# One more probability slot, a down block one score batch later, and a later tangent in a fused attention and mixture-of-experts layer

## The chip, the cores and the metric

The kernel runs on one core of a Trainium2 chip. Its metric is the device time of one launch in microseconds. Before the change it was 2091.04 us (median of 3 runs, 2090.17 to 2092.35).

## What is computed

`x` has 4096 tokens of 256 numbers. `xn` is its layer norm. The output is `x` plus two branches that both read `xn`:

```
# attention, 16 heads of 16
energy = einsum('bqhd,bkhd->bhqk', q, k)          # 4096 x 4096 for each head
attn   = softmax(energy / sqrt(256))
out    = einsum('bhqk,bkhd->bqhd', attn, v)
# feed-forward: one shared expert and, for each token, the best 2 of 8
expert(t) = silu((t @ w1 + b1) * (t @ w3 + b3)) @ w2 + b2      # hidden width 352
```

## The kernel before

**Two streams on one order.** After a front part of about 95 us (norm, projections, routing), TensorE (PE below) runs one order, written out by hand, in which attention and feed-forward are interleaved.

*Attention.* A "group" is one key tile of 128 against 1024 queries: `scores` (L900) issues two matmul instructions for it that fill two of the eight PSUM banks. There are 2048 groups. ScalarE (ACT) takes the exponential of a group from PSUM into one slot of the ring `probs` in SBUF (L1206). A "value step" (`values`, L913) multiplies the two groups of one key tile by the head's values; there are 1024. The scores of three groups fit in PSUM at a time (`SB = 3`, six banks), so the scores of group n wait until group n-3 has left PSUM. For most groups that is the end of exponential n-3. For the places in `MOVED` VectorE (DVE) copies the scores to the slot (L1784), which frees PSUM, and ACT then takes the exponential in place in SBUF (L1198). At the places in `MERGED` one instruction of ACT takes two groups (L1203).

*Feed-forward.* It is cut into 55 "units" of up to 256 tokens: 8 shared, 39 routed, 8 shared. Unit u has three "up" blocks of 12 matmuls (`up_both`, L925), each with two products for a part of the hidden width; DVE adds biases and multiplies them (L1669, L1674). ACT takes one tangent for the unit (`tanh`, L1183), DVE makes `hid` (L1679) and splits it in a rounded part and its rest (L1684 to L1691), and the "down" block (`down_tile`, L937, 18 matmuls) belongs to the next unit's stretch of the order. DVE then takes the result from PSUM (`keep`, L1733 or L1739) and splits the next weights (L1696 to L1708).

**The order of a unit.** `unit(u)` (L1004) has twelve "batches" of three groups' scores. Numbered from 0, batch b holds the places 3b to 3b+2 of the unit. Behind each stands one "gap" of other work. Before the change the gaps are:

batch 0, up; 1, three value steps; 2, up; 3, three value steps; 4, **down of the unit before**; 5, two value steps; 6, two; 7, two; 8, up; 9, two; 10, two; 11, two.

The last group of batches 0, 2 and 5 to 11 is a moved one (`MOVED = (2, 8, 17, 20, ...)`). The groups of batches 1, 3 and 4 are not moved, so the third score of batch 5, place 17, waits for exponential 14. The tangent stands on ACT behind the exponential of place `TANH_AT` - 36 = 5 of the next unit. Units 0 and 1 have no moved and no merged groups, nor do the groups ahead of unit 0 and behind unit 54.

**Slots.** A value step reads two slots, and the slot of a group is written again only when PE has passed its value step. With `NPB = 8` at most eight groups are between scores and values; `FIRST_VALUES` and `FIRST_GROUPS` set the lead at a unit's start.

**Boundaries.** After each 32 value steps the output bank is full: DVE transposes it away (`take_output`, L1628), and the next value step waits for that; two value steps later it adds the result to `resid` (`add_output`, L1633 to L1640). As 18 steps go to a unit, the boundary falls on another place in each: behind `stop` = -(FIRST_VALUES + 18u) mod 32 value steps of unit u, if that is at most 18.

PE, ACT and DVE each run their own list in order, with semaphores between them; none passes a waiting instruction.

## Time and profile before

| | us |
|---|---|
| runs, median (range) | 2091.04 (2090.17 to 2092.35) |
| profiled execution, its own time | 2090.63 |
| its span in the trace | 2088.7 |
| PE, ACT, DVE busy | 2060.6, 2001.1, 1376.5 |
| granted TensorE clock, mean | 1.00 of 2.4 GHz |

The profile is one execution. The page gives busy time by engine, the chain that ended last, and the costliest groups of instructions. The timeline gives each instruction's start and duration from the span's start; equal neighbours are merged in a row (x3). A value step is eight rows of L913 in the trace (x24 is three steps), and a batch of scores is six of L900. How long a block holds PE is read from its start to the start of the next block, since durations overlap.

### The profile page before, as it was taken

How to read it: one execution, taken by the hardware profiler on the slowest of the kernel's cores; microseconds unless marked ns; L12 is line 12 of the kernel's file. 1: busy time of each engine (PE TensorE's matmuls, PEld its weight loads, DVE VectorE, ACT ScalarE, POOL GpSimd, SP SyncE). 2: the span in 40 equal slices, each digit the busy share in tenths (PEclk: the TensorE clock that was granted, in tenths of full speed). 3: DMA queues.
4: the chain of work that ended last, by engine and by line, in shares of the span. 5: the costliest groups of instructions: out<-in, count | busy, mean ns of one | idle time of the engine just before them, and what ended most of it. 6: DMA issues, size and time to landing. Idle time of an engine off the chain costs nothing.

```text
span 2088.7 us, 38791 instructions
## 1 busy us (share of the span) xinstructions
PE 2060.6 (99%) x15722; PEld 968.7 (46%) x15722; DVE 1376.5 (66%) x2038; ACT 2001.1 (96%) x2122; POOL 253.1 (12%) x260
## 2 busy tenths in 40 slices
PE   8999999999999999999999999999999999999998
PEld 6734444444444444444444444444444444444442
DVE  8554666576766666767676767666767665677772
ACT  6799999999999999999999999999999999999998
POOL 0306764000000000000000000000000000033320
PEclk9999999999999999999999999999999999999999
DMA  8874443222231213132222231313132222132322
GB/s 291 287 255 118 119 135 105 61 54 74 60 81 51 79 52 85 52 80 60 66 60 74 62 79 52 86 47 81 52 81 60 73 60 68 57 113 82 112 66 68
DMA packets 223354, 187.83 MB, mean 90 GB/s; under 512 B 110471, under 2 KB 192190, under 8 KB 223174
## 3 DMA queue, kind: packets, MB, share of 16 engines
q1 hardware_dynamic: 209350, 148.68, 25.5%
q0 software_dynamic: 12496, 36.34, 5.4%
q8 instruction: 124, 2.03, 0.4%
q14 instruction: 56, 0.46, 0.1%
q10 hardware_dynamic: 1328, 0.33, 0.1%
HBM read 130.21 MB, written 55.05 MB: 89 GB/s over the span
## 4 chain that ended last, share of the span: by engine, by line
PE 84%; ACT 10%; DVE 4%; DMA 1%; issue 1%; SPq 0%; DVEq 0%; ACTq 0%
PE PS L913 40%; PE PS L900 26%; PE PS L925 12%; ACT probs L1206 6%; PE PS L937 6%; ACT probs L1198 2%; ACT probs L1203 1%; DVE probs L1784 1%; DMA qk_parts<-part_a 1%; DVE stats L1332 0%; DVE probs L1356 0%; DVE o_t L1628 0%; DVE x_parts L1368 0%; PE PS L804 0%; DMA resid<-in_x 0%
## 5 line engine op out<-in xcount | busy, mean ns | idle before, releaser
L1206 ACT ACTIVATE probs<-PS 128x1024 f32<-128x1024 f32 x1359 | 1311.8, 1051 | 49.4 <-PE PS L900 48.4
L913 PE MATMUL PS<-probs,v_head 128*32 128x512 f32 x8192 | 984.5, 599 | 8.4 <-DVE o_t L1628 4.4
L1784 DVE COPY probs<-PS 128x1024 f32<-128x1024 f32 x477 | 583.5, 1223 | 451.3 <-PE PS L900 450.1
L900 PE MATMUL PS<-q_ring,k_stack 50*128 50x512 f32 x4096 | 676.2, 431 | 7.9 <-ACT probs L1206 3.6
L900 PEld LDWEIGHTS PS<-q_ring,k_stack 50*128 50x128 f32 x4096 | 335.0, 184 | 482.7 <-ACT probs L1206 315.0
L1198 ACT ACTIVATE probs<-probs 128x1024 f32<-128x1024 f32 x477 | 517.4, 1085 | 1.5 <-DVE probs L1784 0.8
L913 PEld LDWEIGHTS PS<-probs,v_head 128*32 128x32 f32 x8192 | 210.7, 109 | 521.7 <-issue 391.7
L1203 ACT ACTIVATE probs<-PS 128x2048 f32<-128x2048 f32 x106 | 201.3, 1899 | 0.2 <-PE PS L900 0.2
L925 PE MATMUL PS<-x_hi,w_hi 128*128 128x256 f32 (+9 forms) x660 | 199.2, 302 | 0.0
L1278 POOL DMA_DIRECT2D slot_y<-y_sb x39 | 27.9, 716 | 1378.4 <-DVE y_sb L1739 1342.9
L925 PE MATMUL PS<-x_hi,w_lo 128*128 128x256 f32 (+9 forms) x660 | 184.1, 279 | 0.0
L925 PE MATMUL PS<-x_lo,w_hi 128*128 128x256 f32 (+9 forms) x660 | 183.6, 278 | 0.0
L925 PEld LDWEIGHTS PS<-x_hi,w_hi 128*128 128x128 f32 (+1 forms) x660 | 118.7, 180 | 59.6 <-issue 59.6
L1669 DVE TENSOR_SCALAR gate_in<-PS,bias_sb 128x256 f32<-128x256 f32 (+7 forms) x165 | 76.8, 466 | 90.6 <-PE PS L925 89.1
L925 PEld LDWEIGHTS PS<-x_lo,w_hi 128*128 128x128 f32 (+1 forms) x660 | 118.9, 180 | 0.0
L925 PEld LDWEIGHTS PS<-x_hi,w_lo 128*128 128x128 f32 (+1 forms) x660 | 118.9, 180 | 0.0
L937 PE MATMUL PS<-w_hi,hid_hi 128*128 128x256 f32 (+4 forms) x318 | 95.6, 301 | 0.0
L1700 DVE TENSOR_TENSOR w_lo<-w_raw,w_hi 128x1408 fp32r<-128x1408 f32 x55 | 89.4, 1626 | 1.9
L937 PE MATMUL PS<-w_hi,hid_lo 128*128 128x256 f32 (+4 forms) x318 | 89.7, 282 | 0.0
L937 PE MATMUL PS<-w_lo,hid_hi 128*128 128x256 f32 (+4 forms) x318 | 89.6, 282 | 0.0
L1674 DVE SCALAR_TENSOR_TENSOR prod<-PS,bias_sb,gate_in 128x256 f32<-128x256 f32 (+7 forms) x165 | 76.9, 466 | 5.9
L1269 POOL DMA_INDIRECT slot_x<-y_sb,pos x64 | 67.6, 1056 | 19.1 <-issue 14.6
...
## 6 DMA issues: line engine op xcount, KB each, us to landing
...
```

What stands on the lines that cost most here:

```text
L900: last = pe.matmul(bank(2 * score_buffer(turn, g) + r), k_stack[rows, kt * P:(kt + 1) * P], q_ring[rows, sweep, i * QC:(i + 1) * QC], star ...
L913: last = pe.matmul(bank(O_BANK)[VW * j:VW * (j + 1), :], v_head[:, kt, :], probs[:, slot, (j % 2) * QC:(j % 2 + 1) * QC], start=(kt == 0), ...
L925: last = pe.matmul(f_half(w)[0:FT[j], 0:width(u)], a[u % 2][:, w, dt, j * P:j * P + FT[j]], b[:, dt * CH:dt * CH + width(u)], start=(n == ...
L937: last = pe.matmul(f_half(t)[0:own, :], a[0:rows, j, t * P:t * P + own], b[0:rows, j, :], start=(n == 0), stop=(n == 8))
L1198: nc.scalar.activation(probs[:, prob_slot(g), :], probs[:, prob_slot(g), :], ACT.Exp, scale=ENERGY_SCALE).then_inc(s_exp, 1)
L1203: nc.scalar.activation(pair, bank(2 * score_buffer(h, g), 4), ACT.Exp, scale=ENERGY_SCALE).then_inc(s_exp, 2)
L1206: nc.scalar.activation(probs[:, prob_slot(g), :], bank(2 * score_buffer(h, g), 2), ACT.Exp, scale=ENERGY_SCALE).then_inc(s_exp, 1)
L1269: nc.gpsimd.indirect_dma_start(out=slot_x, out_offset=bass.IndirectOffsetOnAxis(ap=pos[:, u * TPU + t, k:k + 1], axis=0), in_=rows[:, t, : ...
L1669: V.tensor_scalar(gate_in[0:FT[j], 0:width(u)], f_half(0)[0:FT[j], 0:width(u)], bias_sb[0:FT[j], u % 2, j:j + 1], 0.5, ALU.add, ALU.mult). ...
L1674: V.scalar_tensor_tensor(prod[u % 2][0:FT[j], j, 0:width(u)], f_half(1)[0:FT[j], 0:width(u)], bias_sb[0:FT[j], u % 2, 3 + j:4 + j], gate_i ...
L1700: V.tensor_tensor(w13_lo[u % 2][:, :, :, :], w13_raw[:, :, :, :], w13_hi[u % 2][:, :, :, :].bitcast(f32), ALU.subtract).then_inc(s_w13, 1)
L1784: V.tensor_copy(probs[:, prob_slot(g), :], bank(2 * score_buffer(h, g), 2)).then_inc(s_moved, 1)
```

## The change

`NPB` goes from 8 to 9, and the unit begins three groups ahead of twice its value steps instead of two (`FIRST_VALUES` 12, `FIRST_GROUPS` 27). The ring is indexed by a running number; its ninth slot lies in a tile of its own, `probs_8`. The SBUF for it comes from `prod`, whose two buffers now share their middle part, and from `gate_in`, which goes: the first product of an up block is written to its place in `prod` and multiplied there.

The gaps of a unit become: batch 0, up; 1, three value steps; 2, up; 3, three; 4, **two value steps**; 5, **down**; 6, two; 7, two; 8, up; 9, two; 10, two; 11, two. `long_gaps` gives other numbers where a boundary falls behind the second step (two behind batch 1, one behind the up of batch 2, three) or behind the fourth (four, none, two). The tangent goes from behind place 5 to behind place 11, and DVE's list is put in another order. `MOVED` and `MERGED` stay as they are.

```diff
-NPB = 8
+NPB = 9
...
-FIRST_VALUES = 14
-FIRST_GROUPS = 2 * FIRST_VALUES + 2
+FIRST_VALUES = 12
+FIRST_GROUPS = 2 * FIRST_VALUES + 3
 UNIT_VALUES = 18
 UNIT_GROUPS = 2 * UNIT_VALUES
-TANH_AT = 41
+TANH_AT = 47
 MOVED = (2, 8, 17, 20, 23, 26, 29, 32, 35)
 MERGED = (27, 30)
...
+def part_at(u, j):
+
+    return j if u % 2 else (j + 1) % 3
+
+
+def long_gaps(u):
+
+    stop = -(FIRST_VALUES + u * UNIT_VALUES) % NT
+    return (2, 1, 3) if stop == 2 else (4, 0, 2) if stop == 4 else (3, 0, 3)
...
-    return g % NPB
+def prob_slot(n):
+
+    return n % NPB
...
-        probs = sb("probs", [P, NPB, 2 * QC], f32)
+        probs = sb("probs", [P, NPB - 1, 2 * QC], f32)
...
-        gate_in = sb("gate_in", [P, CH], f32)
-        prod = [sb(f"prod{b}", [P, 3, CH], f32) for b in range(2)]
+        prod = sb("prod", [P, 5, CH], f32)
         hid = sb("hid", [P, 3, CH], f32)
+        probs_8 = sb("probs_8", [P, 2 * QC], f32)
...
+        def prob_at(n):
+
+            return probs[:, prob_slot(n), :] if prob_slot(n) < NPB - 1 else probs_8[:, :]
+
+        def prod_of(u):
+
+            return prod[:, 0:3, :] if u % 2 else prod[:, 2:5, :]
...
+                first, late, second = long_gaps(u)
                 next_scores(3)
                 up_both(u, 0)
                 next_scores(3)
-                next_values(3)
+                next_values(first)
                 next_scores(3)
                 up_both(u, 1)
+                next_values(late)
                 next_scores(3)
-                next_values(3)
+                next_values(second)
+                next_scores(3)
+                next_values(2)
                 next_scores(3)
                 if u == 0:
                     count_choices()
                 down_tile(u - 1, 0)
                 down_tile(u - 1, 1)
-                next_scores(3)
-                next_values(2)
                 next_scores(3)
                 next_values(2)
                 next_scores(3)
...
-            next_scores(1)
+            next_scores(2)
...
-            next_scores(1)
...
-                V.tensor_scalar(gate_in[0:FT[j], 0:width(u)], f_half(0)[0:FT[j], 0:width(u)], bias_sb[0:FT[j], u % 2, j:j + 1], 0.5,
+                V.tensor_scalar(prod_of(u)[0:FT[j], part_at(u, j), 0:width(u)], f_half(0)[0:FT[j], 0:width(u)], bias_sb[0:FT[j], u % 2, j:j + 1], 0.5,
                                 ALU.add, ALU.mult).then_inc(s_gin, 1)
...
+                take_values(m + 4)
                 move_scores(u, 8)
                 if real:
                     gate(u, 1)
                     product(u, 1)
-                if u:
-                    hidden(u - 1)
-                take_values(m + 4)
-                if u:
-                    hidden_hi(u - 1)
-                    hidden_lo(u - 1)
-                take_values(m + 6)
                 after_values(m + 4)
                 if more:
                     up_hi(u + 1)
+                take_values(m + 6)
+                if u:
+                    hidden(u - 1)
+                    hidden_hi(u - 1)
+                    hidden_lo(u - 1)
+                take_values(m + 8)
+                move_scores(u, 17)
+                if more:
                     up_lo(u + 1)
                 if u == 0:
                     dve.wait_ge(s_pre, 1)
@@ -1823,12 +1844,10 @@
                     dve.wait_ge(s_prc, 1)
                 else:
                     keep(u - 1)
-                move_scores(u, 17)
                 after_values(m + 6)
+                move_scores(u, 20)
                 if real:
                     down_hi(u)
-                take_values(m + 8)
```

What this moves, for a unit of 256 tokens (unit 31's down block). On PE, where the unit's second gap of three value steps (x12 here, four instructions to a step) and the down block stand, before:

```order
L900 MATMUL PS<-q_ring,k_stack 128x512 x6
L913 MATMUL PS<-probs,v_head 32x512 x12
L900 MATMUL PS<-q_ring,k_stack 128x512 x6
L937 MATMUL PS<-w_hi,hid_hi 128x256
L937 MATMUL PS<-w_lo,hid_hi 128x256
```

and now:

```order
L918 MATMUL PS<-q_ring,k_stack 128x512 x6
L931 MATMUL PS<-probs,v_head 32x512 x12
L918 MATMUL PS<-q_ring,k_stack 128x512 x6
L931 MATMUL PS<-probs,v_head 32x512 x8
L918 MATMUL PS<-q_ring,k_stack 128x512 x6
L955 MATMUL PS<-w_hi,hid_hi 128x256
L955 MATMUL PS<-w_lo,hid_hi 128x256
```

The down block (first row with `hid_hi`) now has one more gap, of two value steps, and one more batch of scores ahead of it.

On ACT, around the tangent (`hid<-prod`), from a moved exponential (`probs<-probs`, place 35 of the unit before) on, before:

```order
L1198 ACTIVATE probs<-probs 128x1024
L1206 ACTIVATE probs<-PS 128x1024 x3
L1183 ACTIVATE hid<-prod 128x768
L1206 ACTIVATE probs<-PS 128x1024 x2
L1198 ACTIVATE probs<-probs 128x1024
L1206 ACTIVATE probs<-PS 128x1024 x8
L1198 ACTIVATE probs<-probs 128x1024
```

and now:

```order
L1217 ACTIVATE probs<-probs 128x1024
L1225 ACTIVATE probs<-PS 128x1024 x5
L1217 ACTIVATE probs<-probs 128x1024
L1225 ACTIVATE probs<-PS 128x1024 x3
L1202 ACTIVATE hid<-prod 128x768
L1225 ACTIVATE probs<-PS 128x1024 x5
L1217 ACTIVATE probs<-probs 128x1024
```

The tangent goes from between exponentials 5 and 6 to between 11 and 12.

On DVE, from the second up block's product on (before) or from the split of the next up weights on (now), before:

```order
L1674 SCALAR_TENSOR_TENSOR prod<-PS,bias_sb,gate_in 128x256
L1679 SCALAR_TENSOR_TENSOR hid<-hid,prod 128x768
L1684 CAST hid_hi<-hid 128x512
L1685 CAST hid_hi<-hid 96x256
L1690 TENSOR_TENSOR hid_lo<-hid,hid_hi 128x512
L1691 TENSOR_TENSOR hid_lo<-hid,hid_hi 96x256
L1696 CAST w_hi<-w_raw 128x1408
L1700 TENSOR_TENSOR w_lo<-w_raw,w_hi 128x1408
L1739 COPY y_sb<-PS 128x512
L1784 COPY probs<-PS 128x1024
L1704 CAST w_hi<-w_raw 128x768
L1784 COPY probs<-PS 128x1024
```

and now:

```order
L1716 CAST w_hi<-w_raw 128x1408
L1699 SCALAR_TENSOR_TENSOR hid<-hid,prod 128x768
L1704 CAST hid_hi<-hid 128x512
L1705 CAST hid_hi<-hid 96x256
L1710 TENSOR_TENSOR hid_lo<-hid,hid_hi 128x512
L1711 TENSOR_TENSOR hid_lo<-hid,hid_hi 96x256
L1804 COPY probs<-PS 128x1024
L1720 TENSOR_TENSOR w_lo<-w_raw,w_hi 128x1408
L1759 COPY y_sb<-PS 128x512
L1804 COPY probs<-PS 128x1024
L1724 CAST w_hi<-w_raw 128x768
L1728 TENSOR_TENSOR w_lo<-w_raw,w_hi 128x768
```

The rounded up weights (`w_hi` 1408 wide) now come ahead of `hid`, the first copy of scores (place 17) ahead of the rest of the up weights (`w_lo`), and both halves of the down weights (768 wide) behind the copy of place 20.

## Rows read from the trace of the kernel before

**Rows 1.** The page: busy time by engine, and the costliest group.

```profile
PE 2060.6 (99%) x15722; PEld 968.7 (46%) x15722; DVE 1376.5 (66%) x2038; ACT 2001.1 (96%) x2122; POOL 253.1 (12%) x260
...
L1206 ACT ACTIVATE probs<-PS 128x1024 f32<-128x1024 f32 x1359 | 1311.8, 1051 | 49.4 <-PE PS L900 48.4
```

**Rows 2.** Windows of units 32, 31, 22: length; busy PE, PEld, DVE, ACT, POOL; clock.

```profile
1245.10:1279.83 34.73, 34.71 (x273) 16.24 (x271) 23.16 (x29) 34.06 (x36) 0.71 (x1) 1.00 0.16 46
1209.32:1245.10 35.78, 34.92 (x273) 16.12 (x271) 24.10 (x33) 34.06 (x36) 0.71 (x1) 1.00 0.26 70
895.50:930.42 34.92, 34.79 (x273) 16.22 (x271) 24.26 (x33) 34.18 (x36) 0.71 (x1) 1.00 0.28 68
```

**Rows 3.** Timeline, PE: unit 32, batches 2 to 6 (start, duration, line, shapes).

```profile
1251.22 0.39 PE L925 MATMUL PS<-x_hi,w_hi 128*128 128x256 f32 x1
...
1252.84 1.03 PE L900 MATMUL PS<-q_ring,k_stack 50*128 50x512 f32 x6
1253.80 2.78 PE L913 MATMUL PS<-probs,v_head 128*32 128x512 f32 x24
1256.51 0.96 PE L900 MATMUL PS<-q_ring,k_stack 50*128 50x512 f32 x6
1257.40 0.39 PE L937 MATMUL PS<-w_hi,hid_hi 128*128 128x256 f32 x1
...
1259.75 0.96 PE L900 MATMUL PS<-q_ring,k_stack 50*128 50x512 f32 x6
...
1262.50 0.96 PE L900 MATMUL PS<-q_ring,k_stack 50*128 50x512 f32 x6
```

**Rows 4.** Timeline, ACT: unit 32, from the tangent to place 15.

```profile
1250.35 0.90 ACT L1183 ACTIVATE hid<-prod 128x768 f32<-128x768 f32 x1
1251.09 2.00 ACT L1206 ACTIVATE probs<-PS 128x1024 f32<-128x1024 f32 x2
...
1257.05 2.86 ACT L1206 ACTIVATE probs<-PS 128x1024 f32<-128x1024 f32 x3 [0.28 <-PE PS L900]
1260.29 1.94 ACT L1206 ACTIVATE probs<-PS 128x1024 f32<-128x1024 f32 x2 [0.38 <-PE PS L900]
```

**Rows 5.** Timeline, PE: unit 32, the gap behind batch 11.

```profile
1276.97 2.03 PE L913 MATMUL PS<-probs,v_head 128*32 128x512 f32 x16
1278.93 0.50 PE L900 MATMUL PS<-q_ring,k_stack 50*128 50x512 f32 x2
```

**Rows 6.** Timeline, ACT: unit 1, which has no moved groups.

```profile
178.30 1.94 ACT L1206 ACTIVATE probs<-PS 128x1024 f32<-128x1024 f32 x2
```

**Rows 7.** Timeline, PE: the same place of unit 1.

```profile
179.59 1.21 PE L900 MATMUL PS<-q_ring,k_stack 50*128 50x512 f32 x6
180.72 0.64 PE L913 MATMUL PS<-probs,v_head 128*32 128x512 f32 x4
```

**Rows 8.** Timeline, DVE: unit 32, `hid` and the up weights; unit 50, `add_output`.

```profile
1253.87 0.95 DVE L1679 SCALAR_TENSOR_TENSOR hid<-hid,prod 128x768 f32<-128x768 f32 x1
...
1256.13 0.41 DVE L1691 TENSOR_TENSOR hid_lo<-hid,hid_hi 96x256 fp32r<-96x256 f32 x1
...
1257.38 1.63 DVE L1700 TENSOR_TENSOR w_lo<-w_raw,w_hi 128x1408 fp32r<-128x1408 f32 x1
...
1903.78 0.24 DVE L1633 RECIPROCAL rec<-o_t 128x16 f32<-128x16 f32 x1
...
1904.52 0.42 DVE L1640 TENSOR_TENSOR resid<-resid,early_sq 128x256 f32<-128x256 f32 x1
```

**Rows 9.** Timeline, PE: unit 31, a boundary inside the second gap of three.

```profile
1219.93 1.92 PE L913 MATMUL PS<-probs,v_head 128*32 128x512 f32 x16 [0.84 <-DVE o_t L1628]
```

**Rows 10.** Timeline, ACT: the tail, tangent and down block of unit 54.

```profile
2050.44 0.91 ACT L1183 ACTIVATE hid<-prod 128x768 f32<-128x768 f32 x1
2051.18 8.43 ACT L1206 ACTIVATE probs<-PS 128x1024 f32<-128x1024 f32 x9
2061.21 1.02 ACT L1206 ACTIVATE probs<-PS 128x1024 f32<-128x1024 f32 x1 [1.61 <-PE PS L900]
```

More of the change, by code:

```diff
@@ L221, in layer_program @@
         krow = sb("krow", [1, P + H], f32)
+        tile_f, tile_r = krow[0:1, 0:ST], krow[0:1, ST:2 * ST]
         qbound = sb("qbound", [P, 2], f32)
@@ L911, in values @@
                 for j in range(QCH):
-                    slot = prob_slot(sweep * GS + 2 * kt + j // 2)
+                    slot = prob_at(h * GH + sweep * GS + 2 * kt + j // 2)
                     last = pe.matmul(bank(O_BANK)[VW * j:VW * (j + 1), :], v_head[:, kt, :],
-                                     probs[:, slot, (j % 2) * QC:(j % 2 + 1) * QC], start=(kt == 0), stop=(kt == NT - 1))
+                                     slot[:, (j % 2) * QC:(j % 2 + 1) * QC], start=(kt == 0), stop=(kt == NT - 1))
                 if kt == NT - 1:
@@ L1182, in tanh @@
                     act.wait_ge(s_hlo, u)
-                nc.scalar.activation(hid[:, :, 0:width(u)], prod[u % 2][:, :, 0:width(u)], ACT.Tanh).then_inc(s_tanh, 1)
+                nc.scalar.activation(hid[:, :, 0:width(u)], prod_of(u)[:, :, 0:width(u)], ACT.Tanh).then_inc(s_tanh, 1)
             for h in range(H):
@@ L1197, in _ @@
                         act.wait_ge(s_moved, moved_up_to(h * GH + g))
-                        nc.scalar.activation(probs[:, prob_slot(g), :], probs[:, prob_slot(g), :], ACT.Exp,
+                        nc.scalar.activation(prob_at(h * GH + g), prob_at(h * GH + g), ACT.Exp,
                                              scale=ENERGY_SCALE).then_inc(s_exp, 1)
@@ L1201, in _ @@
                         act.wait_ge(s_scores, h * GH + (g + 2))
-                        pair = probs[:, prob_slot(g):prob_slot(g) + 2, :].rearrange("p a n -> p (a n)")
+                        pair = probs[:, prob_slot(h * GH + g):prob_slot(h * GH + g) + 2, :].rearrange("p a n -> p (a n)")
                         nc.scalar.activation(pair, bank(2 * score_buffer(h, g), 4), ACT.Exp, scale=ENERGY_SCALE).then_inc(s_exp, 2)
@@ L1205, in _ @@
                         act.wait_ge(s_scores, h * GH + (g + 1))
-                        nc.scalar.activation(probs[:, prob_slot(g), :], bank(2 * score_buffer(h, g), 2), ACT.Exp,
+                        nc.scalar.activation(prob_at(h * GH + g), bank(2 * score_buffer(h, g), 2), ACT.Exp,
                                              scale=ENERGY_SCALE).then_inc(s_exp, 1)
@@ L1673, in product @@
                 dve.wait_ge(s_gin, 3 * u + j + 1)
-                V.scalar_tensor_tensor(prod[u % 2][0:FT[j], j, 0:width(u)], f_half(1)[0:FT[j], 0:width(u)], bias_sb[0:FT[j], u % 2, 3 + j:4 + j],
-                                       gate_in[0:FT[j], 0:width(u)], ALU.add, ALU.mult).then_inc(s_prod, 1)
+                part = prod_of(u)[0:FT[j], part_at(u, j), 0:width(u)]
+                V.scalar_tensor_tensor(part, f_half(1)[0:FT[j], 0:width(u)], bias_sb[0:FT[j], u % 2, 3 + j:4 + j],
+                                       part, ALU.add, ALU.mult).then_inc(s_prod, 1)
             def hidden(u):
                 dve.wait_ge(s_tanh, u + 1)
-                V.scalar_tensor_tensor(hid[:, :, 0:width(u)], hid[:, :, 0:width(u)], 1.0, prod[u % 2][:, :, 0:width(u)], ALU.add, ALU.mult).then_inc(s_hid, 1)
+                V.scalar_tensor_tensor(hid[:, :, 0:width(u)], hid[:, :, 0:width(u)], 1.0, prod_of(u)[:, :, 0:width(u)], ALU.add, ALU.mult).then_inc(s_hid, 1)
             def hidden_hi(u):
                 dve.wait_ge(s_hid, u + 1)
-                own = slice(0, width(u))
-                V.tensor_copy(hid_hi[:, 0:2, own], hid[:, 0:2, own])
-                V.tensor_copy(hid_hi[0:FT[2], 2, own], hid[0:FT[2], 2, own]).then_inc(s_hhi, 1)
+                own, first, last = slice(0, width(u)), part_at(u, 0), part_at(u, 2)
+                V.tensor_copy(hid_hi[:, 0:2, own], hid[:, first:first + 2, own])
+                V.tensor_copy(hid_hi[0:FT[2], 2, own], hid[0:FT[2], last, own]).then_inc(s_hhi, 1)
             def hidden_lo(u):
                 dve.wait_ge(s_hhi, u + 1)
-                own = slice(0, width(u))
-                V.tensor_tensor(hid_lo[:, 0:2, own], hid[:, 0:2, own], hid_hi[:, 0:2, own].bitcast(f32), ALU.subtract)
-                V.tensor_tensor(hid_lo[0:FT[2], 2, own], hid[0:FT[2], 2, own], hid_hi[0:FT[2], 2, own].bitcast(f32),
+                own, first, last = slice(0, width(u)), part_at(u, 0), part_at(u, 2)
+                V.tensor_tensor(hid_lo[:, 0:2, own], hid[:, first:first + 2, own], hid_hi[:, 0:2, own].bitcast(f32), ALU.subtract)
+                V.tensor_tensor(hid_lo[0:FT[2], 2, own], hid[0:FT[2], last, own], hid_hi[0:FT[2], 2, own].bitcast(f32),
                                 ALU.subtract).then_inc(s_hlo, 1)
@@ L1783, in move_scores @@
                 dve.wait_ge(s_scores, n + 1)
-                V.tensor_copy(probs[:, prob_slot(g), :], bank(2 * score_buffer(h, g), 2)).then_inc(s_moved, 1)
-            for half in range(2):
-                V.memset(prod[half][FT[2]:P, 2, :], 0.0)
+                V.tensor_copy(prob_at(h * GH + g), bank(2 * score_buffer(h, g), 2)).then_inc(s_moved, 1)
+            V.memset(prod[FT[2]:P, 2, :], 0.0)
             V.memset(hid_hi[FT[2]:FT[2] + 1, 2, :].bitcast(f32), 1.0)
```

4 lines of the change are left out of this document (removed).

## The prediction

> **What bounds the kernel now.** I read the page first. PE is busy for 2060.6 us of 2088.7 and ACT for 2001.1, with only 49.4 us of idle time ahead of ACT's largest group [rows 1]. Both are close to full, so the shares don't say which of them sets the time. The windows do it for one unit: unit 32 takes 34.73 us, and in it ACT is busy for 34.06 [rows 2]. Then I read the timeline of PE block by block. A batch of scores holds PE for 0.89 us, an up block for 1.62, three value steps for 2.71, the down block for 2.35, and two value steps for 2.75 - 0.89 = 1.86 [rows 3]. Twelve batches, three up blocks, two gaps of three, six of two and the down block are 10.68 + 4.86 + 5.42 + 11.16 + 2.35 = 34.47 us. So PE is behind its own work for all but 0.26 us of the unit. ACT steps on every 0.91 us from one exponential to the next, 0.74 us behind the tangent [rows 4], and 36 groups and a tangent come to about 33.7 us. ACT therefore has 1.0 us to spare in a unit, and the timeline shows where: exponential 12 starts 0.5 us late behind three value steps, exponential 15 as late behind the down block [rows 4]. PE is the bound, and ACT becomes it wherever PE must wait for an exponential before it may write PSUM again.
>
> The reader should keep two constants. When PE comes late, the exponential starts 0.54 us behind the start of its batch (1257.05 against 1256.51, 1260.29 against 1259.75) [rows 3, 4]. When the third score of a batch must wait for the exponential three groups earlier, the next block starts 0.48 us behind that exponential's end: in unit 1 it ends at 180.24 and the values start at 180.72, 1.13 us behind the batch's start instead of 0.89 [rows 6, 7].
>
> **The change part by part.** The matmuls, exponentials and copies stay the same in number, shape and form; the first product written into `prod` and the memset less are worth nothing. So PE's 34.47 us stay, and only waits change.
>
> *Ninth slot.* Behind batch 11 the two value steps hold PE for 1.96 us [rows 5], 0.10 more than elsewhere: with eight slots' lead the second step needs exponential 33, which is just ending. With nine it needs 32. Gain 0.10 a unit.
>
> *Tangent six groups later.* It starts at 1250.35, exactly when exponential 6 would have, and exponential 6 follows at 1251.09 [rows 4]. Batch 2 stands at 1251.22 - 0.89 = 1250.33 [rows 3], so without the tangent exponential 6 could start at 1250.87 at the earliest. The tangent now covers the lateness of exponential 12 (gain), and leaves 0.4 to 0.5 us of it at exponential 6. What PE sees of it: batch 3, which takes 0.96 us [rows 3], waits 0.07 for exponential 7 today and won't; but the 0.10 won behind batch 11 brings batch 1 as near to exponential 1, and I put 0.07 back there.
>
> *Down block one batch later.* This decides. From exponential 6 to the end of 14 ACT has eight exponentials' steps and the tangent: 4.56 (6 to 11) + 0.90 + 0.74 + 1.83 (12 to 14), all steps of 0.91 [rows 4], + 1.05 for its duration [rows 1] = 9.08 us, and it starts 0.54 behind batch 2, so exponential 14 ends 9.62 us behind batch 2. PE's way from batch 2 to batch 5 is 0.89 + 1.62 + 0.89 + 2.71 + 0.89 + 1.86 = 8.86 us. The third score of batch 5 (place 17) waits for exponential 14, since place 14 isn't moved, and the down block starts at 9.62 + 0.48 = 10.10 instead of 8.86 + 0.89 = 9.75. That is 0.35 us of PE's time lost in each unit. Before, batch 5 came behind the down block, 3.24 us after batch 4 [rows 3], and exponential 14 was long over. ACT then has 15, 16 and 17 left and runs dry in the down block for about 0.8 us. The bounds: nothing lost, if ACT has caught up by batch 5 in another way; 0.48, if exponential 12 waits for batch 4 as well.
>
> *DVE's new order.* `hid` needs 2.67 us [rows 8] from the tangent's end (13.05 behind batch 0) and is ready at 15.8, ahead of the down block at 16.2. Then come the copy of place 17, `w_lo` (1.63) [rows 8], `keep` and the copy of place 20, which ends some 5.1 us behind the third score of batch 5; ACT wants it at 5.05. I take 0 for it; late by 0.3 is the other end.
>
> *Sum for a full unit:* -0.10 - 0.07 + 0.07 + 0.35 = +0.25 us, so 34.98 in place of 34.73. Of the 55 units 49 are of this kind (2 to 43 and 48 to 54, without the narrow 44 to 46 and their neighbour's short down block, where ACT is the bound anyway): +12 us.
>
> *Boundaries.* Before, six units (stop 2 and 4: 8, 15, 24, 31, 40, 47) lose 1.05 us each, since the boundary falls inside three value steps and PE waits for the transpose [rows 2, 9]. The new gaps keep it out of every gap. But what takes its place is not free.
> - Units 15, 31, 47 (now stop 6): `add_output` (1.16 us, 1903.78 to 1904.94) [rows 8] stands behind both halves of the down weights and ahead of the copy of place 23. Before, the same cost 0.2 where it fell so (unit 22, 34.92) [rows 2]; that stretch is now 0.7 us later, so I put 1.0. Net 0.
> - Units 8, 24, 40 (now stop 4): four value steps, then batch 4 and the value steps behind it wait for exponentials 11 and 12, 0.9 us, and `add_output` is ahead of the copy of place 20, 1.0 us. Net +0.9 each.
> - Units 13, 29, 45 (now stop 10): the transpose comes behind both halves of the down weights, and the value steps of batch 7 wait, +0.8 each.
> - Units 17, 33, 49 (now stop 2): batch 2 comes 0.86 us earlier and waits for exponential 5, +0.8 each.
> - Others: -2 in all.
> Together 0 + 2.7 + 2.4 + 2.4 - 2 = +5.5 us, the least certain term (-4 to +9).
>
> *Tail.* The last tangent comes three groups later and the last down block four groups earlier. Before, the tangent ended at 2051.35 [rows 10], with `hid` 2.8 us behind it, long ahead of the down block, and ACT idled for 1.61 us by that block alone [rows 10]. Now the down block waits: tangent 1.7 us behind the exponential that frees its batch, then 2.8 for `hid`, against 0.5: 4.0 us for PE, 3.5 for ACT. Units 0 and 1, without moved groups: +1.
>
> Sum: 12 + 5.5 + 3.5 + 1 = +22 us on the profiled 2090.6, which lies 0.4 under the median: 2113 us.
>
> **The rivals.**
>
> *A. The gaps fit, and the kernel gets faster.* If batch 5 does not wait (its third score free in time), the unit loses only 0.17 of its waits or all 0.26, 8 to 13 us in all; the boundaries give 6 more and the tail takes 3.5: about 2078. For it: ACT's idle time lies just at the long gaps, and the two longest are pulled apart. Against it: the 9.62 against 8.86 + 0.41.
> The Trainium skill (Perfetto Trace Analysis, Identifying the Most-Contended Engine) says that matmul busy share is no fair measure and that occupancy is one for ScalarE; by that rule ACT with its 96% is the engine to fill, and a change that spreads its gaps must pay. The trace here agrees that PE's 99% proves nothing, but the block sum of 34.47 in 34.73 shows PE as the bound; by the page alone the sum would be this rival's.
>
> *B. It cancels.* The wait at batch 5 is there but nearer 0.1 us, and the boundaries cost nothing: 5 - 6 + 3.5 - 2, 2091.
>
> *C. DVE is late in every unit.* The copy of place 20 comes 0.3 us late, exponentials 20 to 27 with it, and PE gets that back as a wait at the merged pairs, where it already waits today. It decides once `w_lo` and `keep` end more than 0.1 us later than reckoned. +14: 2127.
>
> **How the numbers follow.** Forecast 0.64, A 0.12, B 0.10, C 0.14. A measurement tells 0.2% (4.2 us) from no change. Slower by more: forecast and C, 0.78; within: B, 0.10; faster: A, 0.12. The range goes from B's lower side, 2088, to 2128, which takes in C; the forecast's own range is 2100 to 2122.
>
> **What would show it.** Right: full units of 34.9 to 35.1 us; batch 5 holding PE for 1.2 to 1.3 us; ACT idle 0.7 to 0.9 us at exponential 18 and 0.3 to 0.5 at 6, none at 12 and 15; 1.86 us behind batch 11; a wait of 4 us ahead of the last down block. Wrong: batch 5 at 0.89 and units under 34.7 (A); the copy of place 20 ending later than exponential 19 (C). The forecast fails first if exponential 14 ends by batch 5's start plus 0.41.

## The result, and the profile after

The changed kernel takes 2117.24 us (median of 4, 2114.95 to 2119.08), the kernel before, run beside it, 2091.64 (2090.17 to 2092.35). The ratio is 1.0124, 95% interval [1.0108, 1.0140]: slower by 26 us. The forecast was 2113 in a range of 2088 to 2128. Of the experiments below, one execution of e10 was slow (6651.57 us) and is left out of its range.

The page of after, busy time by engine, the shares of the chain that ended last, and the largest group:

```profile
span 2116.3 us, 38786 instructions
...
PE 2080.3 (98%) x15722; PEld 973.4 (46%) x15722; DVE 1372.0 (65%) x2037; ACT 2008.7 (95%) x2122; POOL 251.2 (12%) x260
...
PE 60%; ACT 30%; DVE 5%; issue 3%; DMA 1%; SPq 0%; DVEq 0%; ACTq 0%
...
L1225 ACT ACTIVATE probs<-PS 128x1024 f32<-128x1024 f32 x1359 | 1299.9, 1046 | 58.8 <-PE PS L918 57.5
```

Nothing here got dearer by itself: an exponential takes 1046 ns where it took 1051 [rows 1]. PE's busy time rose by 19.7 us without one matmul more, which already says that its records hold waits (some 5 us of it is a lower clock, below). ACT lost 9.4 us more ahead of its exponentials [rows 1]. In the chain that ended last ACT has 30% (10% before). So both engines wait more, each for the other.

Windows over unit 32 (ordinary), 24 (stop 4) and 29 (stop 10) say where; the columns are those of [rows 2]:

```profile
1251.96:1286.92 34.96, 34.87 (x271) 16.22 (x271) 22.34 (x28) 34.19 (x36) 0.71 (x1) 1.00 0.20 51
968.48:1005.44 36.96, 36.16 (x271) 16.19 (x271) 24.21 (x33) 34.30 (x36) 0.71 (x1) 1.00 0.25 68
1145.27:1180.93 35.66, 34.88 (x271) 16.23 (x271) 24.00 (x33) 34.33 (x35) 0.71 (x1) 1.00 0.21 58
```

The ordinary unit went from 34.73 [rows 2] to 34.96. PE's timeline of the same unit, batches 2 to 6, beside [rows 3]:

```profile
1257.17 0.96 PE L918 MATMUL PS<-q_ring,k_stack 50*128 50x512 f32 x6
...
1259.68 0.96 PE L918 MATMUL PS<-q_ring,k_stack 50*128 50x512 f32 x6
...
1263.29 0.96 PE L918 MATMUL PS<-q_ring,k_stack 50*128 50x512 f32 x6
...
1266.03 1.32 PE L918 MATMUL PS<-q_ring,k_stack 50*128 50x512 f32 x6
1267.29 0.39 PE L955 MATMUL PS<-w_hi,hid_hi 128*128 128x256 f32 x1
...
1269.63 0.96 PE L918 MATMUL PS<-q_ring,k_stack 50*128 50x512 f32 x6
```

Batch 5 holds PE from 1266.03 to 1267.29, 1.26 us instead of 0.89: 0.37 lost, in one place. ACT at the same time, beside [rows 4]:

```profile
1257.71 1.94 ACT L1225 ACTIVATE probs<-PS 128x1024 f32<-128x1024 f32 x2 [0.29 <-PE PS L918]
...
1263.19 0.88 ACT L1202 ACTIVATE hid<-prod 128x768 f32<-128x768 f32 x1
1263.92 4.72 ACT L1225 ACTIVATE probs<-PS 128x1024 f32<-128x1024 f32 x5
...
1270.18 1.94 ACT L1225 ACTIVATE probs<-PS 128x1024 f32<-128x1024 f32 x2 [0.46 <-PE PS L918]
```

Exponentials 12 to 16 start from 1263.92 in steps of 0.91, so 14 ends at 1263.92 + 1.82 + 1.05 = 1266.79, and 0.48 later, at 1267.27, PE may go on; it does at 1267.29. ACT is starved at exponential 6 and at 18 and nowhere between. Rival C is out by VectorE's timeline:

```profile
1264.10 0.96 DVE L1699 SCALAR_TENSOR_TENSOR hid<-hid,prod 128x768 f32<-128x768 f32 x1 [2.51 <-ACT hid L1202]
...
1266.36 0.41 DVE L1711 TENSOR_TENSOR hid_lo<-hid,hid_hi 96x256 fp32r<-96x256 f32 x1
...
1270.67 1.22 DVE L1804 COPY probs<-PS 128x1024 f32<-128x1024 f32 x1
```

`hid` is ready at 1266.77, half a microsecond ahead of the down block, and the copy of place 20 ends at 1271.89, as ACT comes to it (exponential 20 starts at 1272.00).

The tail, PE and then ACT, from the last tangent on (before: [rows 10]):

```profile
2073.71 0.90 PE L918 MATMUL PS<-q_ring,k_stack 50*128 50x512 f32 x4
2078.63 0.55 PE L955 MATMUL PS<-w_hi,hid_hi 128*128 128x256 f32 x1 [4.02 <-DVE hid_lo L1711]
...
2082.74 1.93 PE L931 MATMUL PS<-probs,v_head 128*32 128x512 f32 x8
2084.60 0.73 PE L918 MATMUL PS<-q_ring,k_stack 50*128 50x512 f32 x4
```

```profile
2074.71 0.99 ACT L1202 ACTIVATE hid<-prod 128x768 f32<-128x768 f32 x1
...
2085.14 3.77 ACT L1225 ACTIVATE probs<-PS 128x1024 f32<-128x1024 f32 x4 [7.61 <-PE PS L918]
```

The wait of 4.0 us is the forecast one. What was not forecast comes behind it: the down block takes 2082.74 - 2078.63 = 4.11 us where it took 2.35 [rows 3], and one value step 1.86 where its neighbours take 1.0. Windows over the two give the granted clock (the last column but two):

```profile
2078.63:2082.74 4.11, 4.11 (x18) 3.89 (x18) 0.00 (x0) 0.00 (x0) 0.00 (x0) 0.50 0.01 4
2082.74:2084.60 1.86, 1.86 (x10) 0.21 (x10) 0.69 (x1) 0.00 (x0) 0.00 (x0) 0.52 0.00 0
```

0.50 is 1.2 GHz, after 4 us in which PE did nothing. It also fell in the narrow units 44 and 46, whose up blocks are 96 and 32 columns wide (256 in a full unit). Windows over one gap of three value steps in unit 46 (2.71 us elsewhere), and over units 44 and 46:

```profile
1753.29:1757.70 4.41, 4.41 (x27) 1.01 (x25) 1.65 (x6) 3.18 (x5) 0.00 (x0) 0.61 0.01 4
...
1744.73:1781.13 36.40, 35.63 (x262) 15.04 (x262) 18.73 (x27) 33.94 (x37) 0.71 (x1) 0.95 0.22 68
1673.34:1709.35 36.01, 35.47 (x262) 15.20 (x262) 20.64 (x30) 34.04 (x36) 1.43 (x2) 0.95 0.30 87
```

Read from first up block to first up block, the 27.6 us of span lie so:

| stretch | before | after | difference |
|---|---|---|---|
| start to unit 0 | 125.42 | 121.38 | -4.0 |
| units 0, 1 | 72.27 | 72.89 | +0.6 |
| units 2 to 43 | 1465.10 | 1478.98 | +13.9 |
| units 44 to 47 | 138.04 | 143.46 | +5.4 |
| units 48 to 52 | 174.75 | 176.48 | +1.7 |
| units 53, 54 and the end | 113.12 | 123.10 | +10.0 |

The first and the last row belong together: three groups and two value steps that stood ahead of unit 0 now stand behind unit 54.

### The profile page after: what moved, and what is told of

The parts are those of the page before. It is cut to its first block, busy times and chain, and to the rows that moved or that the text cites. A ratio compares the mean times of both kernels' runs of the same rounds, so it can differ in the third digit from the quotient of the medians.

```text
span 2116.3 us, 38786 instructions
## 1 busy us (share of the span) xinstructions
PE 2080.3 (98%) x15722; PEld 973.4 (46%) x15722; DVE 1372.0 (65%) x2037; ACT 2008.7 (95%) x2122; POOL 251.2 (12%) x260
## 4 chain that ended last, share of the span: by engine, by line
PE 60%; ACT 30%; DVE 5%; issue 3%; DMA 1%; SPq 0%; DVEq 0%; ACTq 0%
PE PS L931 27%; ACT probs L1225 22%; PE PS L918 20%; PE PS L943 7%; PE PS L955 5%; ACT probs L1217 4%; ACT probs L1222 2%; ACT hid L1202 2%; DVE probs L1804 1%; DVE w_lo L1720 1%; DMA qk_parts<-part_a 1%; DVE stats L1351 0%; DVE probs L1375 0%; DVE y_sb L1759 0%; DVE w_lo L1728 0%
## 5 line engine op out<-in xcount | busy, mean ns | idle before, releaser
L1225 ACT ACTIVATE probs<-PS 128x1024 f32<-128x1024 f32 x1359 | 1299.9, 1046 | 58.8 <-PE PS L918 57.5
L918 PE MATMUL PS<-q_ring,k_stack 50*128 50x512 f32 x4096 | 696.1, 435 | 15.5 <-ACT probs L1225 6.1
L1217 ACT ACTIVATE probs<-probs 128x1024 f32<-128x1024 f32 x477 | 510.1, 1069 | 10.8 <-DVE probs L1804 9.1
L1699 DVE SCALAR_TENSOR_TENSOR hid<-hid,prod 128x768 f32<-128x768 f32 (+7 forms) x55 | 49.9, 907 | 126.8 <-ACT hid L1202 126.8
L1688 DVE TENSOR_SCALAR prod<-PS,bias_sb 128x256 f32<-128x256 f32 (+7 forms) x165 | 76.8, 466 | 84.2 <-PE PS L943 82.6
L1694 DVE SCALAR_TENSOR_TENSOR prod<-PS,bias_sb,prod 128x256 f32<-128x256 f32 (+7 forms) x165 | 76.9, 466 | 5.9
```

What stands on the lines that cost most here:

```text
L918: last = pe.matmul(bank(2 * score_buffer(turn, g) + r), k_stack[rows, kt * P:(kt + 1) * P], q_ring[rows, sweep, i * QC:(i + 1) * QC], star ...
L1217: nc.scalar.activation(prob_at(h * GH + g), prob_at(h * GH + g), ACT.Exp, scale=ENERGY_SCALE).then_inc(s_exp, 1)
L1225: nc.scalar.activation(prob_at(h * GH + g), bank(2 * score_buffer(h, g), 2), ACT.Exp, scale=ENERGY_SCALE).then_inc(s_exp, 1)
L1688: V.tensor_scalar(prod_of(u)[0:FT[j], part_at(u, j), 0:width(u)], f_half(0)[0:FT[j], 0:width(u)], bias_sb[0:FT[j], u % 2, j:j + 1], 0.5, A ...
L1694: V.scalar_tensor_tensor(part, f_half(1)[0:FT[j], 0:width(u)], bias_sb[0:FT[j], u % 2, 3 + j:4 + j], part, ALU.add, ALU.mult).then_inc(s_p ...
L1699: V.scalar_tensor_tensor(hid[:, :, 0:width(u)], hid[:, :, 0:width(u)], 1.0, prod_of(u)[:, :, 0:width(u)], ALU.add, ALU.mult).then_inc(s_hi ...
```

## The experiments

All ratios are to the kernel before, run beside each. "Unit" is the median full unit away from boundaries.

| | edit | us (median, range) | ratio [95%] | unit |
|---|---|---|---|---|
| e1 | after, tangent back | 2108.48 (2107.13-2108.78) | 1.0079 [1.0063, 1.0094] | 34.95 |
| e2 | ninth slot alone | 2090.66 (2090.30-2092.46) | 0.9996 [0.9987, 1.0005] | 34.73 |
| e3 | after, plain gaps | 2118.44 (2117.95-2121.43) | 1.0133 [1.0117, 1.0148] | 34.96 |
| e4 | e1, place 14 moved | 2090.59 (2090.09-2093.74) | 0.9999 [0.9990, 1.0008] | 34.72 |
| e5 | e4, DVE's order | 2091.72 (2089.90-2093.39) | 1.0004 [0.9995, 1.0013] | 34.70 |
| e6 | e4, no merged pairs | 2094.80 (2093.23-2096.73) | 1.0018 [1.0009, 1.0027] | 34.80 |
| e7 | e5, tangent at 8 | 2106.25 (2105.33-2110.19) | 1.0080 [1.0067, 1.0094] | 34.96 |
| e8 | before, tangent at 8 | 2106.54 (2105.99-2107.85) | 1.0076 [1.0064, 1.0089] | 35.04 |
| e9 | e7, place 11 moved | 2098.79 (2095.69-2099.90) | 1.0029 [1.0018, 1.0041] | 34.60 |
| e10 | e9, `add_output` later | 2097.30 (2093.43-2098.57) | 1.0020 [1.0011, 1.0030] | 34.64 |
| e11 | e9 where it fits, else e5 | 2090.35 (2088.25-2092.38) | 0.9993 [0.9984, 1.0002] | 34.60 |
| e12 | after, PE kept busy in the tail | 2117.23 (2116.33-2118.97) | 1.0119 [1.0103, 1.0134] | 34.98 |

### e1: the tangent back behind place 5

```diff
-TANH_AT = 47
+TANH_AT = 41
```

> The changed kernel with the tangent back behind place 5 of the next unit (TANH_AT 41), all else as changed. Theory W (the third score of batch 5 waits for exponential 14, wherever the tangent stands): exponential 12 is then late again behind three value steps, exponential 14 ends 3.42 us behind batch 4, the third score of batch 5 still waits, 0.26 us instead of 0.36, and batch 3 waits 0.07 again: full units 34.85 to 34.95 (now 34.95). Only the tail changes, where the down block no longer waits for the hidden part: 6 us less. Time 2107 to 2112. Rival T (the tangent's new place is what costs): full units fall to 34.7, time 2097 to 2100.

PE, the second up block's neighbours and batch 5 of unit 32:

```profile
1256.99 1.09 PE L918 MATMUL PS<-q_ring,k_stack 50*128 50x512 f32 x6
1258.01 2.78 PE L931 MATMUL PS<-probs,v_head 128*32 128x512 f32 x24
...
1263.47 1.20 PE L918 MATMUL PS<-q_ring,k_stack 50*128 50x512 f32 x6
```

Batch 3 now holds PE for 1.02 us and batch 5 for 1.13: the same loss, split over two places, and a unit of the same length. So the later tangent is not what an ordinary unit pays for. It is paid in the tail, where unit 53 to the end takes 117.1 us instead of 123.1, 6.0 us, and the down block is at full clock again; and in the units with stop 4, which fall from 36.95 to 36.20: in unit 24 the two value steps behind batch 4 take 1.85 us instead of 2.21, and batch 5 0.90 instead of 1.27. That makes up the 2.1 us by which the profiled executions differ in units 2 to 43. Units 0 and 1 give 1.0.

### e2: the ninth slot and the lead alone

`NPB`, `FIRST_VALUES`, `FIRST_GROUPS` and the buffers of after; the down block, the gaps, the tangent and DVE's order of before (against after, DVE's list not shown):

```diff
-    return (2, 1, 3) if stop == 2 else (4, 0, 2) if stop == 4 else (3, 0, 3)
+    return 3, 0, 3
...
                 next_scores(3)
-                next_values(2)
-                next_scores(3)
                 if u == 0:
                     count_choices()
                 down_tile(u - 1, 0)
                 down_tile(u - 1, 1)
+                next_scores(3)
+                next_values(2)
                 next_scores(3)
                 next_values(2)
```

> The ninth slot and the three groups' lead alone: down block back behind batch 4, gaps 3 and 3 always, tangent and DVE's order as in the kernel before. Theory W: as before, but the two value steps behind batch 11 take 1.86 us instead of 1.96: full units 34.63, and seven units with a boundary inside three steps instead of six: 2086 to 2088. Rival S (the ninth slot, the shared middle of prod or the longer lead cost something themselves): 2091 or more.

```profile
1247.14 0.96 PE L918 MATMUL PS<-q_ring,k_stack 50*128 50x512 f32 x6
...
1249.65 1.08 PE L918 MATMUL PS<-q_ring,k_stack 50*128 50x512 f32 x6
1250.66 2.78 PE L931 MATMUL PS<-probs,v_head 128*32 128x512 f32 x24
```

The gap behind batch 11 is 1.85, as reckoned, and the unit stays 34.73: batch 3 holds PE for 1250.66 - 1249.65 = 1.01 instead of 0.96, and batch 1 for 0.93. The 0.10 that the slot gives comes back at the next two places where a score waits for an exponential. Missed by 3 to 5 us.

### e3: plain gaps of three

```diff
-    return (2, 1, 3) if stop == 2 else (4, 0, 2) if stop == 4 else (3, 0, 3)
+    return 3, 0, 3
...
-                take_values(m + 4)
                 move_scores(u, 8)
                 if real:
                     gate(u, 1)
                     product(u, 1)
+                take_values(m + 4)
```

> The changed kernel with gaps of three and three value steps in every unit (no long_gaps). The adapted units cost 36.95 us (three of them) and 35.65 (three), 2.0 and 0.7 over a full unit of 34.95; a boundary inside three steps cost 1.05. Theory W: the first three gain 0.9 each, the others lose 0.35: 2115 to 2117. Rival G (the adapted gaps save the 1.05 us of a boundary as meant): 2121 to 2124.

Missed on both sides: the 2118.44 us lie between the two expectations, and the units with stop 4 did not gain the 0.9 each that theory W gave them. Units with stop 2 take 36.05 us instead of 35.65, those with stop 4 37.0 instead of 36.95. The adapted gaps are worth 0.4 us in three units and nothing in the other three. With (4, 0, 2) the stall of 1.05 inside the gap goes, and comes back as 0.49 at batch 4 and 0.36 inside the gap behind it, of two steps.

### e4: place 14 moved as well

```diff
-TANH_AT = 47
+TANH_AT = 41
-MOVED = (2, 8, 17, 20, 23, 26, 29, 32, 35)
+MOVED = (2, 8, 14, 17, 20, 23, 26, 29, 32, 35)
...
+                if u:
+                    hidden(u - 1)
+                    hidden_hi(u - 1)
+                    hidden_lo(u - 1)
                 after_values(m + 4)
                 if more:
                     up_hi(u + 1)
                 take_values(m + 6)
-                if u:
-                    hidden(u - 1)
-                    hidden_hi(u - 1)
-                    hidden_lo(u - 1)
-                take_values(m + 8)
-                move_scores(u, 17)
+                move_scores(u, 14)
                 if more:
                     up_lo(u + 1)
+                take_values(m + 8)
+                move_scores(u, 17)
```

> As e1_tangent_back, and place 14 is a moved one too: DVE copies its scores, so the third score of batch 5 waits for the copy and not for exponential 14; DVE makes hid first and w_lo stands between the copies of 14 and 17. Theory W: batch 5 holds PE 0.89 us, full units 34.55 to 34.65, 2092 to 2097 with the rest of the losses left. Rival D (DVE or ACT sets the pace here anyway, and another copy of 1.22 us a unit only moves the wait): full units 34.85 or more, 2106 or more.

A window over unit 32, and PE's batches 3 and 5 in it:

```profile
1242.43:1277.14 34.71, 34.71 (x273) 16.30 (x271) 23.64 (x29) 34.10 (x37) 0.72 (x1) 1.00 0.19 50
```

```profile
1250.21 1.10 PE L918 MATMUL PS<-q_ring,k_stack 50*128 50x512 f32 x6
...
1256.70 0.96 PE L918 MATMUL PS<-q_ring,k_stack 50*128 50x512 f32 x6
```

This is the experiment that settles the cause in the ordinary unit. With PSUM freed by VectorE at place 14, batch 5 costs 0.89 and the unit is back at 34.72, though the down block still stands one batch later, behind a gap of two steps. Against after, 0.36 went at batch 5 and only 0.24 was won, because with the tangent back behind place 5 batch 3 waits (1.03); so the unit missed the 34.55 to 34.65 expected. Against e1, which has the tangent at the same place, 0.24 went at batch 5 and 0.23 was won: this wait did not come back elsewhere, and ACT runs dry behind it, at exponential 15, for 0.33 us.

The total, 2090.59, is the time of before, but not by this wait alone. The profiled execution is 18.3 us shorter than e1's: 9.6 in units 2 to 43, 1.5 in units 48 to 52, 0.5 behind them, and 6.6 in units 44 to 47, which take 136.7 us here, at full clock.

### e5: VectorE's order at the boundaries

```diff
                 after_values(m + 4)
+                take_values(m + 6)
                 if more:
                     up_hi(u + 1)
-                take_values(m + 6)
                 move_scores(u, 14)
...
-                after_values(m + 6)
                 move_scores(u, 20)
+                after_values(m + 6)
                 if real:
                     down_hi(u)
+                take_values(m + 10)
+                move_scores(u, 23)
                 if real:
                     down_lo(u)
                 if u == 0:
                     counts()
                 after_values(m + 8)
-                take_values(m + 10)
-                move_scores(u, 23)
```

> As e4_move14, with DVE's order changed where a boundary makes it late: the transpose ahead of the up weights, the transpose of stop 10 and the copy of place 23 ahead of the rest of the down weights (w_lo), add_output behind the copy of 20. Theory B (what the changed kernel pays at boundaries is DVE's order): units 13, 29, 45 fall from 0.8 over a full unit to 0.1, units 15, 31, 47 from 1.4 to 0.3, the rest as e4: 2083 to 2086. Rival P (boundaries cost what PE's order makes them cost): as e4, 2090 to 2092.

Units with stop 10 fell from 35.50 to 34.77 and those with stop 4 from 35.90 to 35.09, so the 0.7 to 0.8 us that went was VectorE's order and not PE's gaps; stop 4 keeps 0.4. Stop 6 kept 0.8 to 0.9 (0.3 was expected). The new order also has a price: units 22 and 38 (stop 8) rose from 34.72 and 34.76 to 35.47 and 35.61, and units 20 and 36 (stop 12) by 0.27. In unit 22 the rest of the down weights now stands behind the copy of place 23, and with `add_output` next to it the copy of place 26 starts 24.94 us into the unit instead of 24.09. Units 2 to 43 got shorter by 2.9 us, but the total did not, against the 2083 to 2086 expected: in the profiled execution unit 45 took 35.42 us instead of 34.20, in one gap of two value steps (3.49 us where it is 2.05), and the stretch behind it 1.9 more.

### e6: no merged exponentials

```diff
-MERGED = (27, 30)
+MERGED = ()
```

> As e4_move14 without merged exponentials (MERGED empty): each pair becomes two exponentials, 1.82 us for 1.77, and PE no longer waits for a pair's end behind batches 9 and 10 (0.09 us a unit). Theory L (from the down block to batch 3 of the next unit ACT's chain is the bound, and a wait taken from PE in that stretch comes back later in it): units get longer by ACT's 0.05 to 0.1 per pair, 34.8 to 34.9 instead of 34.72, 2096 to 2100. Rival M (PE loses at the merged pairs themselves): units of 34.62, 2085 to 2087.

The gaps behind batches 9 and 10 fall to 1.85, as they must without the merged instructions, and the unit does not get shorter but longer, 34.80: batch 1 rises from 0.94 to 1.15 in unit 32. That is e2 again. Between the down block and batch 3 of the next unit ACT runs without a break, and its chain, not any one wait, has a length; what leaves one waiting place turns up at the next. M is out, and 34.80 is the unit that L expected. The cost, 4 us, is under the 6 to 9 that L expected.

### e7 and e8: the tangent behind place 8

```diff
-TANH_AT = 41
+TANH_AT = 44
```

This is e7 against e5, and e8 against the kernel before.

> As e5_dve_order with the tangent behind place 8 (TANH_AT 44). It leaves the stretch in which ACT is the bound (down block to exponential 7) and goes where ACT would run dry at exponential 12. Theory L: batch 3 stops waiting for exponential 7 (0.10 us), full units 34.55 to 34.65, 2077 to 2081. Rival M: the wait only moves to batch 4 or 5, time as e5.

> The kernel before with the tangent three groups later alone (TANH_AT 44). Theory L: batch 3 takes 0.89 us instead of 0.96, full units 34.65 to 34.68, 2087 to 2089. Rival H (hid comes too late for the down block behind batch 4, or the freed 0.07 is lost elsewhere): 2091 or more.

Both missed, by 26 and 18 us, in one and the same way. ACT and PE of e7, unit 32:

```profile
1254.63 1.94 ACT L1225 ACTIVATE probs<-PS 128x1024 f32<-128x1024 f32 x2 [0.29 <-PE PS L918]
...
1257.40 0.84 ACT L1202 ACTIVATE hid<-prod 128x768 f32<-128x768 f32 x1
1258.13 4.68 ACT L1225 ACTIVATE probs<-PS 128x1024 f32<-128x1024 f32 x5
```

```profile
1256.60 0.97 PE L918 MATMUL PS<-q_ring,k_stack 50*128 50x512 f32 x6
...
1260.21 1.33 PE L918 MATMUL PS<-q_ring,k_stack 50*128 50x512 f32 x6
1261.47 1.92 PE L931 MATMUL PS<-probs,v_head 128*32 128x512 f32 x16
```

Batch 3 waits no longer (0.89), but batch 4 takes 1.26. Its third score waits for exponential 11, which is not moved; 11 ends at 1258.13 + 1.82 + 1.05 = 1261.00, and 0.47 later PE goes on. In e8 it is batch 4 ahead of the down block:

```profile
1265.77 1.33 PE L900 MATMUL PS<-q_ring,k_stack 50*128 50x512 f32 x6
1267.04 0.39 PE L937 MATMUL PS<-w_hi,hid_hi 128*128 128x256 f32 x1
```

Exponentials 9 to 14 start there from 1263.70 on, so 11 ends at 1263.70 + 1.82 + 1.05 = 1266.57, and PE goes on 0.47 later. It is the wait of after, one batch earlier, and one rule fits all three kernels: the last place of a batch that is not moved is a fence for the next batch's third score, and a tangent between a starved exponential and the fence is paid there.

### e9: place 11 moved as well

e7 with 11 in `MOVED`, its copy ahead of `hidden`, and `up_hi`, `up_lo` each behind a copy:

```diff
+                move_scores(u, 11)
                 if u:
                     hidden(u - 1)
...
-                if more:
-                    up_hi(u + 1)
                 move_scores(u, 14)
                 if more:
-                    up_lo(u + 1)
+                    up_hi(u + 1)
                 take_values(m + 8)
                 move_scores(u, 17)
+                if more:
+                    up_lo(u + 1)
```

> As e7_tangent_at_8 with place 11 moved as well as 14, its copy ahead of hid on DVE, the copy of 14 ahead of the up weights and w_lo behind the copy of 17. Theory F (each unmoved last place of a batch is a fence: the next batch's third score waits for its exponential, and the tangent, wherever it stands between exponential 6 and such a place, is paid there): e7 pays 0.36 us at batch 4 for exponential 11; with 11 and 14 moved there is no fence between batch 3 and the down block, and batches 3, 4 and 5 take 0.89: full units 34.5 to 34.6, 2080 to 2086. Rival D (two more copies of 1.22 us and hid, one after the other, make DVE late, and a copy or the down block waits): full units 34.8 or more, 2095 or more.

```profile
1242.08:1276.68 34.60, 34.60 (x273) 16.20 (x271) 24.43 (x30) 34.12 (x36) 0.72 (x1) 1.00 0.20 51
```

```profile
1249.82 0.97 PE L918 MATMUL PS<-q_ring,k_stack 50*128 50x512 f32 x6
...
1253.42 0.96 PE L918 MATMUL PS<-q_ring,k_stack 50*128 50x512 f32 x6
...
1256.19 0.96 PE L918 MATMUL PS<-q_ring,k_stack 50*128 50x512 f32 x6
```

With no fence left, batches 3, 4 and 5 all hold PE for 0.89 to 0.90 and the ordinary unit is the shortest of all, 34.60. That half was right. The total was not (2080 to 2086 expected): units with stop 6 take 36.4 and 36.5, where e5 has 35.5 and 35.6, since the transpose now stands behind the copy of place 11 and the whole of `hid`:

```profile
1216.92 0.96 PE L918 MATMUL PS<-q_ring,k_stack 50*128 50x512 f32 x6
1218.82 1.92 PE L931 MATMUL PS<-probs,v_head 128*32 128x512 f32 x16 [0.94 <-DVE o_t L1647]
```

Stop 2 takes 36.1 to 36.2 (35.4 in e5), and units 44 and 46 ran in part at the lower clock (35.77 and 37.45 us).

### e10 and e11: two attempts to keep the 34.60

e10 is e9 with `after_values(m + 8)`, which adds the output, behind `move_scores(u, 26)` instead of ahead of `join(u, 1)`.

> As e9_move_11_14, with add_output of the units with stop 6 behind the copy of place 26 instead of behind the copy of place 23. Theory: those units (15, 31, 47) lose 0.8 us today because add_output makes the copy of place 26 and the next ones late; they lose 0.2 then, 2 us less than e9. Rival (their loss is PE's order): as e9.

Units with stop 6 fell by 0.56 each, to 35.82 and 35.93; the median is 1.5 us under e9's, where 2 were expected, and the intervals of the two overlap.

e11 takes e9's pattern only in units 3 to 42 whose stop isn't 2, 4 or 6, and e5's elsewhere:

```diff
+def plain(u):
+
+    return MOVE_FROM < u < 43 and -(FIRST_VALUES + u * UNIT_VALUES) % NT not in (2, 4, 6)
...
-    return MOVE_FROM <= u < MOVE_TO and place in MOVED
+    return MOVE_FROM <= u < MOVE_TO and (place in MOVED or place == 11 and plain(u))
```

> e9_move_11_14's pattern (place 11 moved, tangent behind place 8) only in the 32 full units of 3 to 42 whose boundary isn't at stop 2, 4 or 6; everywhere else e5_dve_order's. e9 showed 34.60 us for such a unit and e5 34.71, but e9 lost 0.7 to 1.0 us more in each unit with stop 2, 4 or 6, and more in the narrow units where the granted clock fell. Theory: both gains add, 32 x 0.11 = 3.5 us under e5: 2087 to 2089, the first version under the kernel before. Rival: where one pattern follows the other, or where the clock falls in other units, it is lost again: 2091 or more.

Units 2 to 43 take 1461.7 us, 3.4 less than in the kernel before, but units 53 to the end 117.7 against 113.1, with only 3.7 of that given back ahead of unit 0. 2090.35 us, at a ratio of 0.9993 [0.9984, 1.0002], is the lowest median measured; it is not told apart from before, and the 2087 to 2089 expected did not come.

### e12: PE kept busy in the tail's wait

32 matmuls into a bank whose content nobody reads, behind the last product's release:

```diff
             next_scores(2)
+            pe.wait_ge(s_prod, 3 * UNITS)
+            for n in range(32):
+                pe.matmul(f_half(0)[:, :], w13_hi[(UNITS - 1) % 2][:, 0, 0, 0:P], x_hi[:, 0:CH], start=True, stop=True)
             down_tile(UNITS - 1, 0)
```

> The changed kernel with 32 idle matmuls (128 x 128 on 256 columns, into the bank that the last down block then overwrites; 3.7 us) while PE waits for hid ahead of the last down block. In the changed kernel that block took 4.11 us instead of 2.35, and the value step behind it 1.86 instead of 1.00, at a granted clock of 0.50 of full speed. Theory C (the clock fell because PE stood idle): the clock stays at 1.00, the block takes 2.35, 2.6 us less in the tail: 2113 to 2115. Rival (the block is slow for another reason, or the clock falls anyway): as the changed kernel, 2117.

```profile
2077.93 4.10 PE L1075 MATMUL PS<-x_hi,w_hi 128*128 128x256 f32 x32
...
2084.34 1.07 PE L931 MATMUL PS<-probs,v_head 128*32 128x512 f32 x8
```

```profile
2082.03:2084.34 2.31, 2.31 (x18) 2.18 (x18) 0.00 (x0) 0.00 (x0) 0.00 (x0) 1.00 0.00 0
1745.21:1784.17 38.96, 38.41 (x263) 15.79 (x261) 18.74 (x27) 34.18 (x37) 0.72 (x1) 0.87 0.21 64
```

With PE at work through the wait the clock stays at 1.00, the block takes 2.31 and the value step 1.00; units 53 to the end are 2.6 us shorter (120.5 against 123.1), the size expected. The time is another matter: the median, 2117.23 us, is after's, where 2113 to 2115 were expected. In the profiled execution the 2.6 us were lost again in the narrow units (146.1 us against 143.5, unit 46 at a granted clock of 0.87); no profile shows whether the other three runs lost them there too.
The Trainium skill (TensorE: Matmul & The Clock Gate, HAM oscillation — how this bites in real kernels) says that a wait of PE, there for a DMA, can throttle it to half clock, so that the next burst starts cold. The tail agrees, with a wait for `hid`: 4.11 us against 2.31 for the same 18 matmuls.

## Why the prediction was right, step by step

**The wait at batch 5: right in place, cause and size.** 0.36 of PE's time in each unit, for exponential 14; unit 34.96 for 34.98. e4 takes the fence away and nothing else of the down block's new place, and the unit's loss goes. The signs named ahead of the result came, one of them smaller: ACT dry at exponential 18 for 0.5 us, where 0.7 to 0.9 were forecast (17 ends three steps, 2.73, behind 14, and 18 can start 0.48 + 2.35 + 0.54 = 3.37 behind it, so the forecast's own terms give 0.64), and at 6 for 0.3, none at 12 and 15, 1.85 us behind batch 11. Rivals A and B needed batch 5 nearer to 0.9, C a late copy; none came.

**The ninth slot and the tangent's 0.07: right as events, wrong as terms.** In the sum they were a gain of 0.10 and a shift of 0.07 that cancels. e2 measures the 0.10 at nothing: batches 1 and 3 take it back. Waits that end on the same uninterrupted run of ACT can't be added up one by one. In after it did no harm, for the forecast of the unit stood on the block sum between two starved exponentials, where the arithmetic closes. It did harm in the expectations of e2 and e4, which added the places again.

**Boundaries: right.** Stop 4 came to 2.0 us over the unit (forecast 1.95), stop 6 to 0.8 to 0.95 (1.0), stop 10 to 0.7 to 0.8 (0.8), stop 2 to 0.7 (0.8). Units 2 to 43 got longer by 13.9 us; 42 times 0.24 is 10.1, and 3.8 are left for the boundaries there. I called this the least certain term, and named VectorE's order as the price. The runs confirm that whole for stop 10 (e5) and in part for stop 4: of its 2.0 us VectorE's order is 0.8 (e5 against e4), the later tangent 0.75 (e1), and 0.4 stay in e5.

**The narrow units: the step that failed.** "Where ACT is the bound anyway" cost them at nothing, and they cost 5.4 us, of which only unit 45's boundary (0.8) stood in the sum. In unit 45, at full clock, 1.1 us are the boundary at batch 7. In units 44 and 46 the value steps took 0.97 and 1.70 us longer, at a window clock of 0.95 in each. The remaining 1.6 can't be laid on single places. The fence is there too (batch 5 takes 1.13), but before, the same units waited 0.8 to 0.9 us at batch 5, behind their short down block, and now they wait at batches 7, 8 and 9 instead.

**The tail: the wait right, its price short by the clock.** 4.0 us of wait were forecast and came. The half clock behind it added 1.76 for the down block and 0.86 for a value step; e12 confirms 2.6 of it. Front and tail with units 48 to 52 come to +7.7, where 3.5 and seven units at 0.25 with one boundary (0.8) make 6.0.

With the two together, 5.4 - 0.8 + 2.6 = 7.2 us are outside the forecast; the difference in span was 27.6 against 22, since the other terms were together 1.6 too high.

**Open.** Why the clock falls in narrow units is not settled. It fell in the profiled executions of after (44, 46), e1 (44, 46), e3 (46), e5 (45), e6 (46), e9 (44, 46), e10 (46) and e12 (45, 46), and not in before, e2, e4, e7, e8 and e11, though PE's records have it busy for over 35 of 36 us in after's units 44 and 46. Of these 15 falls 14 began 1.6 to 3.3 us behind the start of a narrow up block (96, 64 or 32 columns), and the other one behind a wait of 1.58 us (e12, unit 45). But the six kernels without a fall run the same narrow blocks, so the block alone does not do it. Kernels that differ in one constant differ in it, so that some us of a total here can be this and not the edit. No run isolates it.
